# Last batches, expert weights, the choice of bins and the clearing of bins in a fused graph, Mamba and expert kernel

## What is computed

```python
h = relu(adj @ layernorm(x) @ gcn_w + gcn_b);  h = layernorm(h) * ln_g + ln_b
xc, z = split(h @ w_in);  u = silu(causal_conv4(xc) + conv_b)
dt, B, C = split(u @ w_xp);  dt = softplus(dt @ w_dt + b_dt)
for t in rows:                        # 256 channels x 16 states
    state = exp(dt[t] * A) * state + dt[t] * B[t] * u[t];  y[t] = state @ C[t]
x = x + ((y + u * D) * silu(z)) @ w_out
H = gelu(layernorm(x) @ W1 + b1)      # 128 -> 512
p = softmax(H @ Wg + bg);  e = argmax(p)       # 8 experts
x = x + p[e] * (H @ Wd[e] + bd[e])    # each row with its own expert
```

## Time and profile before

| what | us |
|---|---|
| median of 3 runs (1882.68 to 1887.48) | 1887.21 |
| the profiled execution | 1887.13 |
| its span, first to last instruction | 1885.3 |
| VectorE busy | 1557.7 (83%) |
| TensorE busy | 1534.3 (81%) |
| GpSimd busy | 978.9 (52%) |
| ScalarE busy | 846.2 (45%) |

### The profile page before, as it was taken

How to read it: one execution, slowest core, us unless ns; L and a number is a source line. 1 busy time by engine, 2 the same in 40 slices (tenths; PEclk the granted TensorE clock), 3 DMA queues, 4 the chain that set the end, 5 groups by cost and what they waited for, 6 DMA issues and landing times. The chain is left out here.

```text
span 1885.3 us, 18148 instructions
## 1 busy us (share of the span) xinstructions
PE 1534.3 (81%) x4568; PEld 770.3 (41%) x4568; DVE 1557.7 (83%) x2103; ACT 846.2 (45%) x1500; POOL 978.9 (52%) x553
## 2 busy tenths in 40 slices
PE   6799888898989898998989898999899866345554
PEld 2343334444434444444435353544444433223342
DVE  8016999999998999999898989999989999996221
ACT  2033445454446373645464544546363645444211
POOL 0002443545455574747474756666574747586444
PEclk9899998999998999998988999999989886656777
DMA  8899997978776878787787878788868754242232
GB/s 302 296 311 391 379 347 276 328 264 313 260 287 232 307 269 307 261 310 281 274 284 273 283 272 285 270 285 283 270 238 311 260 178 139 94 146 79 82 99 50
DMA packets 155792, 479.52 MB, mean 254 GB/s; under 512 B 19477, under 2 KB 45602, under 8 KB 155698
## 3 DMA queue, kind: packets, MB, share of 16 engines
q1 hardware_dynamic: 139954, 428.59, 64.7%
q0 software_dynamic: 14592, 45.77, 7.5%
q10 hardware_dynamic: 1152, 4.19, 0.6%
HBM read 447.88 MB, written 33.75 MB: 255 GB/s over the span
## 5 line engine op out<-in xcount | busy, mean ns | idle before, releaser
L987 PE MATMUL ps_adj<-ring,nodes 128*128 128x512 f32 x2048 | 964.0, 619 | 86.0 <-DMA ring<-adj 53.5
L440 POOL TENSOR_TENSOR h_c<-hidden,bc_ring 128x1024 f32<-128x1024 f32 x256 | 601.8, 2351 | 783.6 <-DVE inject L916 706.7
L779 DVE TENSOR_TENSOR_SCAN hidden<-decay,state,inject 128x512 f32<-128x512 f32 x512 | 627.6, 1268 | 54.0 <-ACT decay L524 22.9
L987 PEld LDWEIGHTS ps_adj<-ring,nodes 128*128 128x128 f32 x2048 | 397.7, 199 | 610.2 <-issue 481.7
L524 ACT ACTIVATE decay<-dt_sb,negA 128x512 f32<-128x512 f32 x512 | 339.4, 711 | 1.2 <-DVE dt_sb L839 1.0
L916 DVE TENSOR_TENSOR inject<-dtu_sb,bc_ring 128x1024 f32<-128x1024 f32 x256 | 314.4, 1228 | 22.1 <-DMA bc_ring<-bc_dram 14.8
L863 DVE TENSOR_TENSOR y_sum<-y_sum,h_c 128x1024 f32<-128x1024 f32 x224 | 273.5, 1221 | 23.1 <-POOL h_c L440 21.7
L517 ACT COPY state<-hidden 128x2 f32<-128x2 f32 x256 | 49.4, 193 | 535.3 <-DVE hidden L779 534.8
L411 POOL DMA_INDIRECT out<-o_sb,out_at x72 | 85.2, 1183 | 68.3 <-DVE dest L795 22.4
L401 POOL DMA_INDIRECT wd_ring<-wd_rows,wd_at x72 | 105.3, 1462 | 16.6 <-issue 13.6
L406 POOL DMA_INDIRECT got<-bins,row_at x72 | 92.2, 1280 | 18.3 <-issue 16.5
(11 more groups left out here) (166 smaller groups left out, 1360.6 us busy)
## 6 DMA issues: line engine op xcount, KB each, us to landing
ring<-adj SPq DMA_DIRECT2D x512, 512.0 KB, 5.6
bc_ring<-bc_dram SPq DMA_DIRECT2D x256, 512.0 KB, 5.7
bins<-nodes SPq DMA_DIRECT2D x96, 172.0 KB
nodes<-x_rows ACTq DMA_DIRECT2D x8, 512.0 KB, 12.2
x_tile<-x_rows SPq DMA_DIRECT2D x16, 256.0 KB, 5.3
wd_rows<-Wd SPq DMA_DIRECT2D x8, 256.0 KB, 5.0
wd_ring<-wd_rows,wd_at POOLq DMA_INDIRECT x72, 6.3
got<-bins,row_at POOLq DMA_INDIRECT x72, 3.8
```

Source lines behind the costliest of these rows:

```text
L440: nc.gpsimd.tensor_tensor(h_c[:, s % 2], hidden[:, s % 2], over_halves(bc_ring[:, s % BC_RING, 1]), ALU.mult).then_inc(hc_ready, 1)
L779: scan = nc.vector.tensor_tensor_scan(hidden[:, s % 2, h], decay[:, s % 2, h], inject[:, h], state[:, h, s:s + 1], ALU.mult, ALU.add)
L987: last = nc.tensor.matmul(ps_adj[:, 0], nodes[:, m], ring[:, g % RING, m % GROUP], start=(m == 0), stop=(m == J - 1))
```

## The change

Four edits are made together.

1. The clearing of bins moves from bodies -1, 0, 1 (one transfer of 1376 bytes a partition behind each group) to bodies 0 and 1 (two of 1032 bytes a partition behind each group, 128 in all). The layout of the expert weights moves from body -1, group 0 to body 2, two transfers behind each fourth group. The wait for the spare record moves to slot 6 of the batch.
2. The expert weights are no longer gathered by GpSimd with 128 addresses. `control` gives the expert's number (`owner`), SyncE loads it into a register (`value_load`) and issues an ordinary transfer from `wd_rows[expert]`, four for a batch, behind group 14 of the body, after waits for the table, the choice and the use of the buffer two batches ago. In the last batches SyncE does it for each batch, when the choice is made.
3. The choice takes 13 operations in the bodies and 20 in the last batches. Gone are `rem`, the product and sum for `owner`, and `wd_at`; a fused operation takes the place of the comparison, and a bitwise and of `row_at` gives `owner`.
4. In the last batches GpSimd gathers the records of batch `f` before it scatters the outputs of `f-2`; the outputs of the last two batches are scattered at the end.

```diff
-    FILLS = 3 * GROUPS
+    FILLS = 4 * GROUPS
...
-            def expert_rows():
-                rows = wd_rows.ap().rearrange("(e p) (k c) -> e p k c", e=EXPERTS, k=5)
-                for e in range(EXPERTS):
-                    sp.dma_start(rows[e, :, 0:4], Wd[:, :, e]).then_inc(table_in, 16)
-                    sp.dma_start(rows[e, :, 4], bd[e:e + 1, 0].broadcast_to([P, P])).then_inc(table_in, 16)
-                sp.wait_ge(start_c, 13)
-                sp.dma_start(bins.ap()[SPACE:], got[0:1, 0, 0]).then_inc(zero_in, 16)
+            def expert_row(e):
+                sp.dma_start(wd_rows.ap()[e, :, 0:4], Wd[:, :, e]).then_inc(table_in, 16)
+                sp.dma_start(wd_rows.ap()[e, :, 4], bd[e:e + 1, 0].broadcast_to([P, P])).then_inc(table_in, 16)
+                if e == 0:
+                    sp.wait_ge(start_c, 10)
+                    sp.dma_start(bins.ap()[SPACE:], got[0:1, 0, 0]).then_inc(zero_in, 16)
...
+            def load_experts(r):
+                for j in range(PICKS):
+                    e = sp.value_load(owner[0:1, r, j:j + 1], min_val=0, max_val=EXPERTS - 1)
+                    sp.dma_start(wd_ring[:, r, j], wd_rows.ap()[bass.ds(e, 1)].rearrange("a p k c -> p (a k) c")
+                                 ).then_inc(wd_in[r], 16)
...
-                        if isinstance(i, int) and i == -1 and g == 0:
-                            sp.wait_ge(node_ready, 8)
-                            expert_rows()
-                        if isinstance(i, int) and -1 <= i < 2:
-                            clear_bins((i + 1) * GROUPS + g)
+                        if isinstance(i, int) and i in (0, 1):
+                            if (i, g) == (0, 0):
+                                sp.wait_ge(node_ready, 8)
+                            for n in range(2):
+                                clear_bins((2 * i + n) * GROUPS + g)
+                        if isinstance(i, int) and i == 2 and g % 4 == 0:
+                            expert_row(g // 4)
+                    if g == 14 and batch:
+                        chosen_, freed_ = c.value(ctrl_step, -4, 13), c.value(by_done, -6, PICKS)
+                        sp.wait_ge(table_in, 16 * 2 * EXPERTS)
+                        if freed_ is not None:
+                            sp.wait_ge(by_done, freed_)
+                        sp.wait_ge(ctrl_step, chosen_)
+                        load_experts(p)
...
+            for f in range(FLUSH):
+                k = BATCHES + f
+                Count(sp, k).wait(by_done, -2, PICKS)
+                sp.wait_ge(flush_step, 20 * f + 20)
+                load_experts(k % 2)
...
-                    if batch and s in (5, 8, 9):
-                        for j in {5: (0, 1), 8: (2,), 9: (3,)}[s]:
-                            gather_weights(p, j)
...
-                c.wait(o_ready, -2, PICKS + 1)
-                pool.wait_ge(flush_step, 23 * f + 23)
-                c.wait(by_done, -2, PICKS)
                 if f == 0:
                     pool.wait_ge(scat_in, 16 * BLOCKS * TILES)
+                if f >= 2:
+                    c.wait(o_ready, -2, PICKS + 1)
+                pool.wait_ge(flush_step, 20 * f + 20)
                 for j in range(PICKS):
                     gather_rows(k % 2, j)
+                if f >= 2:
+                    for j in range(PICKS):
+                        scatter_out(k % 2, j)
+            for f in (FLUSH - 2, FLUSH - 1):
+                k = BATCHES + f
+                Count(pool, k).wait(o_ready, 0, PICKS + 1)
                 for j in range(PICKS):
-                    gather_weights(k % 2, j)
-                if f:
-                    c.wait(o_ready, -1, PICKS + 1)
-                    for j in range(PICKS):
-                        scatter_out((k - 1) % 2, j)
-            c.wait(o_ready, 0, PICKS + 1)
-            for j in range(PICKS):
-                scatter_out(k % 2, j)
+                    scatter_out(k % 2, j)
...
-                nc.vector.tensor_tensor(rem[:], tail[:], head[:], ALU.subtract).then_inc(mark, 1)
+                nc.vector.tensor_tensor(cand[:], over_picks(head[:]), offset[:], ALU.add).then_inc(mark, 1)
                 after(1)
-                nc.vector.tensor_tensor(has[:], over_picks(rem[:]), (some_at if flush else full_at)[:], ALU.is_ge
-                                        ).then_inc(mark, 1)
-                nc.vector.tensor_tensor(cand[:], over_picks(head[:]), offset[:], ALU.add).then_inc(mark, 1)
+                nc.vector.scalar_tensor_tensor(out=has[:], in0=cand[:], scalar=float(EXPERTS * (1 if flush else P)),
+                                               in1=over_picks(tail[:]), op0=ALU.add, op1=ALU.is_le
+                                               ).then_inc(mark, 1)
...
-                nc.vector.tensor_tensor(weigh[:], chosen[:], over_turns(owner[:]), ALU.mult).then_inc(mark, 1)
...
-                nc.vector.reduce_sum(first_f[:, 1], weigh[:], AX).then_inc(mark, 1)
...
-                nc.vector.tensor_scalar(wd_at[:, r], first_f[:, 1], lane[:, 0:1], None, ALU.add).then_inc(mark, 1)
...
+                nc.vector.tensor_scalar(owner[:, r], row_at[:, r], EXPERTS - 1, None, ALU.bitwise_and
+                                        ).then_inc(mark, 1)
```

More of the change, by code:

```diff
@@ L417, in body @@
                 q = 1 - p
-                for per in (1, 4, 5, 6, 16, 64):
+                for per in (1, 4, 5, 6, 13, 16, 64):
                     c.times_of(per)
@@ L427, in body @@
                         c.wait(id_step, -2, 1)
-                    if batch and s == 5:
-                        pool.wait_ge(table_in, 16 * 2 * EXPERTS)
-                        c.wait(ctrl_step, -4, 16)
-                        c.wait(by_done, -6, PICKS)
                     if batch and s == 6:
+                        pool.wait_ge(zero_in, 16 + 16 * FILLS)
+                        c.wait(ctrl_step, -4, 13)
                         c.wait(scat_in, -2, 16 * BLOCKS)
@@ L724, in control @@
+                nc.vector.tensor_scalar(row_at[:, r], first_f[:, 0], lane8[:, 0:1], None, ALU.add).then_inc(mark, 1)
                 after(11)
-                nc.vector.reduce_sum(first_f[:, 1], weigh[:], AX).then_inc(mark, 1)
-                if not flush:
-                    nc.vector.tensor_scalar(row_at[:, r], first_f[:, 0], lane8[:, 0:1], None, ALU.add
-                                            ).then_inc(mark, 1)
-                after(13)
-                nc.vector.tensor_scalar(wd_at[:, r], first_f[:, 1], lane[:, 0:1], None, ALU.add).then_inc(mark, 1)
@@ new lines, in control @@
+                nc.vector.tensor_scalar(row_at[:, r], row_at[:, r], SPACE - 1, None, ALU.bitwise_and
+                                        ).then_inc(mark, 1)
+                if flush:
+                    nc.vector.tensor_tensor(left[:], over_picks(tail[:]), cand[:], ALU.subtract).then_inc(mark, 1)
+                    after(14)
+                    nc.vector.tensor_tensor(weigh[:], chosen[:], over_turns(left[:]), ALU.mult).then_inc(mark, 1)
+                    after(13)
+                    nc.vector.tensor_scalar_add(first_f[:, 0], row_at[:, r], -float(SPACE)).then_inc(mark, 1)
+                    after(15)
+                    nc.vector.reduce_sum(first_f[:, 1], weigh[:], AX).then_inc(mark, 1)
+                    after(17)
+                    nc.vector.tensor_scalar(first_f[:, 1], first_f[:, 1], need[:, 0:1], None, ALU.is_ge
+                                            ).then_inc(mark, 1)
```

67 lines of the change are left out of this document (18 added, 49 removed).

## The result

The changed kernel takes 1874.93 us (median of 7 runs, 1871.01 to 1884.42) where the kernel before takes 1887.21 us (7 runs on the same chip, 1881.46 to 1889.53): ratio 0.9946, 95% interval 0.9923 to 0.9969. On another chip the same comparison gave 0.9972 (0.9949 to 0.9995). So the change gains 2 to 12 us by the medians, where 29 were forecast. The profiled execution took 1874.40 us, with a span of 1872.6 against 1885.3.

A forecast was written before the change was run, and what follows sets the result against it. VectorE was taken to bound the bodies with a scan, something else what lies ahead. 13.4 - 1 + 4.8 + 9 - 3 + 5.9 = 29.1 us off 1887.13 gave 1858.0 us, range 1844 to 1877.

The forecast's parts named there:

- The start: Ahead of body 0: without layout and clearings in body -1, TensorE's idle time goes; gain 13.4 us.
- Body 0: Larger clearings load the full DMA engines and eat the lead of `bc_ring` transfers; loss 1 us, bounds 0 and 7.
- The choice: Bodies 4 to 15: three fewer VectorE operations save 0.4 us a body, 4.8 us in all.
- GpSimd: Bodies 4 to 15, slot 6: without weight gathers ahead of `h_c`, `y_sum` waits less; 0.75 us a body, 9 us.
- SyncE's hold: Bodies 4 to 15, behind group 14: four register loads and issues hold SyncE 6.6 us, mostly hidden; 3 us charged.
- the allowance of 4.5 us for group 15: Body 6, slot 7: group 15 may be issued 4.5 us late at no cost to TensorE.
- The rival in which the hold undoes all: Bodies 4 to 15: register loads over 2.1 us each cancel all savings; 1908 us at 2.5 us; chance 0.08.
- The last batches: After the bodies: record gathers start earlier behind the choice; 0.3 us plus three rounds of 1.85, gain 5.9 us.
- the mild hold: Bodies 4 to 15: register loads of 1.6 to 1.9 us cost 10 to 24 us, about 1873 us; chance 0.10.
- the bodies keep their length: TensorE or the decay wait takes VectorE's savings at slots 1 and 7; gain 18.3 us, 1869 us; chance 0.13.

The follow-up runs named there:

- the layout alone: Kernel before with only the 16 transfers of the weights' layout moved from ahead of body -1 to body 2; 1878.81 us, ratio 0.9920.
- the old clearing: Changed kernel with 96 clearings, one behind each group of bodies -1, 0 and 1, as in the kernel before; 1874.39 us, ratio 0.9888.
- the mended kernel: Changed kernel with slot 6's product ahead of the waits, records landed before last batches' weights, 96 clearings over bodies -1, 0, 1; 1852.77 us, ratio 0.9797.
- the records first: Changed kernel where SyncE, in the last batches, waits for the landed records before it loads weights; 1868.67 us, ratio 0.9883.
- the later load: The mended kernel with SyncE's weights loaded before group 22 of the body instead of 14; 1857.19 us, ratio 0.9850.

## Why the prediction was wrong, point by point

**The start: right.** 13.4 us forecast, 14.4 measured; the layout alone does it (143.88). VectorE's wait for the first broadcast rows is 13.07 us where it was 13.79, which agrees with the half microsecond that I added for them; over the traces the two clearings overlap here (12.8 to 13.8 us with the new one, 13.5 to 13.8 with the old).

**Body 0: right mechanism, wrong size.** I took 1 us between 0 and 7; it is 3.0 in this trace (2.0 and more in the others), the transfers at 395 GB/s with 2.3 us of waits for `bc_ring`, and 0.7 more ahead of body 0. The bound from the slots' bytes, 0.4 us in each of the seven slots ahead of the convolution, gave 2.8, and the lead that I set against it wasn't there. With the old clearing it is gone. The Trainium skill ("DMA: Bandwidth & Descriptors", "Where 436 GB/s comes from") has a limit of about 358 GB/s per core, half of what two cores share; by it the 36.0 MB of this body (395 GB/s in 91.09 us) would take 100 us. The trace doesn't agree with it as a limit for a core that runs alone, as here: 395 over the whole body.

**The choice: right.** 0.4 a body forecast, 0.47 measured (0.45 to 0.50 over the bodies).

**GpSimd: this step failed.** "At slot 5 two weight gathers ... stand ahead of `h_c` of slot 6 ... I take 0.75 us a body ... 9 us. What is late next is `inject`, VectorE's own." Late next was the landing of the scatters of slot 4, for which GpSimd waits at the head of slot 6, in the code that I had before me. The waits for the product over the run fell by 1.1 us (21.7 to 20.6), not 9. The rows that I read showed `h_c` right behind the gathers with no idle time, and I took the gathers for all that stood there; a wait that ends while its engine is busy leaves no row. The row of body 12 at 1370.90, with its 0.48 us for the scatters, was there to be read. With the wait behind the product the 9.6 us came, and with GpSimd's weights in the mended kernel they went again (21.9 against 11.1): the size was right, the cover was missed.

**SyncE's hold: right in kind, too large in size.** 6.6 us forecast, 5.2 measured (load 0.70 for 1.2, issue 0.61 for 0.45), hidden, at 0.75 us in body 4, which is what the allowance of 4.5 us for group 15 leaves of 5.2; from 600 to 1460 us 4.5 us more of waits for `ring`, while waits for ScalarE behind it fell from 23.2 to 15.0. I charged 3 us, and no trace asks for more. The rival in which the hold undoes all is out.

**The last batches: the second step that failed.** "Then as before 6.66 us to the transpose": it was 8.8 and 8.1 us in the next two rounds and 11.7 in the one behind them (9.5 there before). I had asked whether the weights come in time and not what they do to the records that start with them. 5.9 us forecast, -2.0 measured; with the records first 113.7 became 105.8, 5.9 us under the kernel before, the forecast's figure: 0.4, 1.6, 2.4 and 1.5 us in the first four steps, for 0.3 and three times 1.85.

**Not in the prediction at all.** The turns of the loop (4.9 us in the profiled run) and 1.9 us between the last scatter's issue and the end. For the turns the register loads are shown to be the condition, but not how they act; for the 1.9 us no cause is shown. Rivals had no place for either.

The sum with what was measured: 14.4 - 0.7 - 3.0 at the start; 5.2 for eleven choices, -0.1 for the product's waits (18.8 and 18.9 us in these bodies; the 1.1 of the run lie outside them), -4.9 for the turns and 2.0 of other waits, 1.4 of them decay, in the bodies 4 to 14 (2.2 in all); 2.4 in bodies 1 to 3; 1.2 - 2.0 - 1.9 at the end: 12.6 us, the difference of the spans but for rounding. By its number the closest rival was the mild hold, at 1873, which is chance: a load took 0.70 us and not 1.6 to 1.9, and the hold was hidden. By what happened it was that the bodies keep their length, at 1869, though not for its reason: no other engine became the bound. The decay waits didn't take the savings, as I had it (22.9 us, now 21.5, in bodies 4 to 14). That 1874.9 lies inside the range of 1844 to 1877 is no merit of it, since the terms that missed were a wait and a landing that it had not counted.

## What to carry to other kernels

When work is taken out ahead of an operation, read from the code every wait that its engine passes between the removed work and that operation, and date each one's release: a wait that ended under cover of the removed work is the next bound. When a transfer moves to another queue, ask what starts at the same moment; transfers of two queues that start together landed later here (6.7 us became 8.8), and the one that is needed first should be let land first. Try the parts of a change alone: here one moved block of transfers was worth all that the whole brought, and three small moves of waits and transfers turned 0.5% into 2.0% (on two chips; on a third, with the later load, 0.3% into 1.5%).

## What the hardware showed that was not expected

- A register load on SyncE, with the address that it feeds, took 0.70 us beside its transfer's issue of 0.61 us, and with four such loads a body VectorE's turn of the loop took 4.72 us on average instead of 2.63 (24 turns in 8 kernels against 18 in 6), with SyncE's transfers the same.
- Four indirect gathers of 128 records took 6.6 to 6.8 us from first issue to use, and 8.1 and 8.8 with four 320 KB transfers of another queue issued in the same microsecond (8.0 to 10.0 in the same two rounds of the four other traces that have both).
- A scatter of records by GpSimd in mid-body released its waiter 6.9 us after the end of its issue (545.58 to 552.49), and 5.5 to 7.4 in the eight bodies that wait for it, with SyncE's four weight transfers issued in the same stretch. It isn't theirs alone: the kernel before shows 6.6 us in body 12 without them.
- In every kernel with the weights on SyncE's queue, with register loads or without, 16.1 to 16.2 us lie between the last finish and the end of the span; in every one with GpSimd's (the kernel before, the layout alone, both with gathered weights) it is 14.3. No row explains the 1.9 us.
